# A four-engine state-space kernel: more products on POOL, a convolution tap and ScalarE's long pieces in other places

## What is computed

```python
h = layernorm(x) * (1 + ca) + sa
h, gate = split(h @ in_proj.T)                     # 2 x 1024 channels
h = silu(conv1d_causal(h, 4 taps) + conv_b)
dt, B, C = split(h @ x_proj.T)                     # 128, 16, 16
dt = softplus(dt @ dt_proj.T + dt_b)
A = -exp(A_log)
s[t] = s[t-1] * exp(dt[t] * A) + dt[t] * h[t] * B[t]     # for 1024 x 16 states
y = (sum over n of s[t] * C[t] + h * D) * silu(gate)
x = x + ga * (y @ out_proj.T)
x = x + gb * ((layernorm(x) * (1 + cb) + sb) @ sum(factors) / sqrt(8) + bias)
```

## Time and profile before

| | |
|---|---|
| device time, 3 runs | 2012.16, 2017.43, 2019.25; median 2017.43 us |
| the profiled execution | 2014.19 us, its span 2012.5 us |
| DVE busy | 1861.3 us, 92%, 2219 instructions |
| POOL busy | 1823.4 us, 91%, 757 instructions |
| PE busy | 1768.9 us, 88% |
| ACT busy | 1537.4 us, 76% |
| DMA | 93 GB/s in the mean, 16 engines under a third busy |

### The profile page before, as it was taken

One profiled execution on the slowest core, in us unless ns is written; L12 is line 12 of the kernel. 1 busy time (PEld: TensorE's weight loads), 2 busy tenths in 40 slices (PEclk: granted clock), 3 DMA queues, 4 the chain that ended last, 5 costly groups with the idle time before them and its releaser, 6 DMA issues. The chain is left out here.

```text
span 2012.5 us, 29641 instructions
## 1 busy us (share of the span) xinstructions
PE 1768.9 (88%) x9128; PEld 1316.4 (65%) x9128; DVE 1861.3 (92%) x2219; ACT 1537.4 (76%) x4897; POOL 1823.4 (91%) x757
## 2 busy tenths in 40 slices
PE   7986888989888898988989898898988889898798
PEld 5665757667576765757666675766757676575664
DVE  2798999999999999999999999999999999999995
ACT  3766778797877869778787877878787786977763
POOL 1789999999999999999999999999989999999993
PEclk9897999999999999999999999999999999999899
DMA  5655514032140412304042240403214041220300
GB/s 172 236 121 148 148 42 157 22 126 74 52 138 24 140 47 95 105 22 157 22 143 68 111 137 26 157 22 127 73 58 132 28 139 46 95 79 23 126 27 32
DMA packets 72003, 186.19 MB, mean 93 GB/s; under 512 B 6818, under 2 KB 8482, under 8 KB 63908
## 3 DMA queue, kind: packets, MB, share of 16 engines
q1 hardware_dynamic: 68148, 176.95, 25.8%
q0 software_dynamic: 3696, 7.34, 2.2%
HBM read 172.20 MB, written 12.06 MB: 92 GB/s over the span
## 5 line engine op out<-in xcount | busy, mean ns | idle before, releaser
L596 POOL TENSOR_TENSOR ub<-u,b_all 128x2048 f32<-128x2048 f32 x255 | 1167.8, 4579 | 47.1 <-DMA b_all<-bc_scratch 47.1
L752 ACT ACTIVATE decay<-dt,decay_rate 128x256 f32<-128x256 f32 (+1 forms) x2048 | 880.7, 465 | 6.0 <-DVE state_p L1503 5.4
L1503 DVE TENSOR_TENSOR_SCAN decay<-decay,carry,ub 128x512 f32<-128x512 f32 x589 | 735.5, 1275 | 11.5 <-ACT decay L752 10.5
L614 POOL TENSOR_TENSOR state_p<-state_p,c_all 128x1024 f32<-128x1024 f32 (+1 forms) x256 | 529.8, 2070 | 103.3 <-ACT carry L736 79.0
L1503 DVE TENSOR_TENSOR_SCAN state_p<-decay,carry,ub 128x512 f32<-128x512 f32 x435 | 538.3, 1269 | 38.9 <-ACT decay L752 38.4
L1070 PE MATMUL y_bank<-ident,sc_d 128*128 128x128 f32 x2356 | 351.6, 282 | 94.3 <-DVE sc_d L1518 94.3
L1518 DVE TENSOR_TENSOR sc_d<-decay,c_all 128x512 f32<-128x512 f32 x589 | 378.1, 677 | 13.1 <-PE y_bank L1070 4.4
L1070 PEld LDWEIGHTS y_bank<-ident,sc_d 128*128 128x128 f32 x2356 | 279.4, 145 | 143.3 <-DVE sc_d L1518 131.7
L1070 PE MATMUL y_bank<-ident,state_p 128*128 128x128 f32 x1740 | 247.1, 283 | 106.9 <-POOL state_p L614 105.3
L1070 PEld LDWEIGHTS y_bank<-ident,state_p 128*128 128x128 f32 x1740 | 204.2, 145 | 203.6 <-POOL state_p L614 148.0
L736 ACT ACTIVATE carry<-decay 128x2 f32<-128x2 f32 x589 | 96.4, 164 | 313.3 <-DVE sc_d L1518 313.3
(11 more groups left out here) (141 smaller groups left out, 1837.9 us busy)
## 6 DMA issues: line engine op xcount, KB each, us to landing
win_h<-win_m SPq DMA_DIRECT2D x128, 256.0 KB, 2.6
win_z<-win_m SPq DMA_DIRECT2D x128, 256.0 KB, 2.9
b_all<-bc_scratch SPq DMA_DIRECT2D x31, 1024.0 KB, 4.7
c_all<-bc_scratch SPq DMA_DIRECT2D x31, 1024.0 KB, 5.4
xa<-x SPq DMA_DIRECT2D x16, 512.0 KB, 5.1
xc<-x SPq DMA_DIRECT2D x16, 512.0 KB, 3.8
out<-xc SPq DMA_DIRECT2D x15, 512.0 KB, 3.8
ffn<-factors POOLq DMA_DIRECT2D x7, 1024.0 KB, 9.9
```

The costliest lines, as they stand in the source:

```text
L596: pool.tensor_tensor(ub[:, slot, :, :, :], u[:, (PAIRS * c + q) % U_PAIRS, :, :].unsqueeze(1).to_broadcast([P, QUAD, 2, ROWS]), b_all[:, n ...
L614: pool.tensor_tensor(part, part, c_all[:, n:n + k, :].unsqueeze(2).to_broadcast([P, k, 2, ROWS]), ALU.mult).then_inc(pooled, 1)
L752: last = act.activation(bk[:, j * ROWS + j:(j + 1) * ROWS], dt[:, pair % DT_PAIRS, j, j:], ACT.Exp, scale=decay_rate[:, e, n:n + 1])
L1503: dve.tensor_tensor_scan(dst, bk[:, :], ub[:, quad % UB_RING, i, :, :].rearrange("p j r -> p (j r)"), carried_in[:, n, 2 * q:2 * q + 1], A ...
```

## The change

Three things, and nothing else moves.

1. `EVERY_POOL` gives POOL two units instead of one in quads 7 and 15 of chunks 2 to 15 (28 units in all). DVE has 561 products instead of 589, and 28 of POOL's products are 128x1024 instead of 128x512.
2. In chunks 1 to 14 the two tap instructions of pair 0 stand between the two scans of step 6 instead of at the end of step 5.
3. On ACT the two instructions of `z_after` stand at either side of `decays(43)` and those of `z_before` at either side of `decays(61)`; the two calls of `modulate_after` move half a step back each, and `copy_dt` one step.

```diff
-EVERY_POOL = (2, 2, 2, 1) * PAIRS
+EVERY_POOL = (2, 2, 2, 1, 2, 2, 2, 2) * (PAIRS // 2)
...
-            def normalize(c, nrm, src, dst, chain, done):
+            def normalize(c, t, nrm, src, dst, chain, done):
                 act.wait_ge(chain, NORMS * c + NORMS)
-                for t in range(LB):
-                    last = act.activation(dst[:, t, :], src[:, t, :], ACT.Identity,
-                                          bias=nrm[:, 1, t:t + 1], scale=nrm[:, 0, t:t + 1])
-                last.then_inc(done, 1)
+                made = act.activation(dst[:, t, :], src[:, t, :], ACT.Identity,
+                                      bias=nrm[:, 1, t:t + 1], scale=nrm[:, 0, t:t + 1])
+                if t == LB - 1:
+                    made.then_inc(done, 1)
...
                     decays(2 * step)
...
-                        if s == 21:
+                        if s == 22:
                             copy_dt(c + 1)
...
+                    if lc is not None and s == 21:
+                        z_after(c - 1, 0)
                     if lc is not None and s == 23:
-                        modulate_after(c - 1, 1)
+                        act.wait_ge(mods_made, 4)
+                        modulate_after(c - 1, 0)
+                    if c + 2 < CHUNKS and s == 30:
+                        z_before(c + 2, 0)
...
                     decays(2 * step + 1)
...
                     if c + 2 < CHUNKS and s == 30:
-                        z_before(c + 2)
+                        z_before(c + 2, 1)
                     if lc is not None:
                         if s == 21:
-                            z_after(c - 1)
-                        if s == 22:
-                            act.wait_ge(mods_made, 4)
-                            modulate_after(c - 1, 0)
+                            z_after(c - 1, 1)
+                        if s == 23:
+                            modulate_after(c - 1, 1)
...
                     scan(unit)
...
+                    if la is not None and c and s == 6:
+                        taps(c + 1, 0)
...
                     scan(unit + 1)
...
-                        if a in TAP_AT[c > 0]:
+                        if a in TAP_AT[c > 0] and (c == 0 or s != 5):
                             taps(c + 1, TAP_AT[c > 0][a])
```

More of the change, by code:

```diff
@@ L769, in modulate, with z_before @@
                 return last
-            def z_before(c):
-                normalize(c, nrm_a, xa, xa, norm_a, z_a)
+            def z_before(c, t):
+                normalize(c, t, nrm_a, xa, xa, norm_a, z_a)
             def modulate_before(c, j):
@@ L921, in tanh_gate_last, with z_after @@
                 act.activation(tanh_s[:, :], bank_a[q % 2][:, :], ACT.Tanh, scale=0.5).then_inc(tanh_g_made, 1)
-            def z_after(c):
-                if c + 2 < CHUNKS:
+            def z_after(c, t):
+                if t == 0 and c + 2 < CHUNKS:
                     act.wait_ge(tapped, PAIRS * (c + 3))
-                normalize(c, nrm_c, xc, z2, norm_c, z_c)
+                normalize(c, t, nrm_c, xc, z2, norm_c, z_c)
             def modulate_after(c, j):
@@ L947, in _ @@
             act.activation(cond_s[:, :, :], cond[:, :, :], ACT.Tanh, scale=0.5).then_inc(cond_tanh, 1)
-            z_before(0)
+            for t in range(LB):
+                z_before(0, t)
             act.wait_ge(consts_made, 2)
@@ L1006, in one_round @@
                         if c == 0 and s == 3:
-                            z_before(1)
+                            for t in range(LB):
+                                z_before(1, t)
                         if a == M_AT[c > 0]:
```

## The result

The changed kernel takes **2029.51 us** in the median of 5 runs (2026.95 to 2030.8); the kernel before, 2014.84 in the median of 5 (2012.16 to 2019.25). The ratio is 1.0074, 95% interval 1.0062 to 1.0085: 0.7% slower. The forecast was 2026.6 us, +9.2 us of change against the +14.7 that the medians now show. The profiled execution has a span of 2027.8 us, 15.3 more than the one of before. TensorE's mean granted clock is 0.955 of full speed there, 0.969 before.

A forecast was written before the change was run, and what follows sets the result against it. A loop of waits over POOL, PE, ACT and DVE bounds the kernel, no single engine. Terms +17.0, -9.2 and +1.4 sum to +9.2 us: 2026.6 us against the median 2017.43, 0.46% slower; range 2020 to 2032.

The forecast's parts named there:

- What ends last: DVE's scan of unit 12 hangs on POOL's product of quad 15, over PE and ACT; DVE's way ends within 0.09 us.
- A: Stretch from POOL's product of quad 12 at step 26 to DVE's scan of unit 12: claimed +1.42 us, 12 times.
- first rival: POOL's product isn't what ends last; DVE's way decides, each chunk shrinks by 1.50 us: 1998 us, chance 0.17.
- B: Stretch from DVE's scan of unit 12 to POOL's next product of quad 12: claimed -0.71 us, 13 times.
- B, the tap, +0.78: Between unit 12's scan and step 8, the tap no longer runs inside DVE's wait for the decay: +0.78 us a chunk.
- second rival: The tap is free because some other DVE wait moves behind step 6: 2016.5 us, no difference, chance 0.20.
- Quad 7, -0.62: Around steps 14 to 16, DVE loses unit 29's product, saving 0.79 us, of which 0.62 come through packed PE.
- ACT, -0.87: In steps 22 and 23, DVE's waits of 0.69 and 0.18 us for decays go: -0.87 us a chunk.
- third rival: ACT's gain doesn't come while both costs stay, since `copy_dt` lies behind unit 44's decay: 2038 us, chance 0.10.
- last stretch: After chunk 14's product of quad 12: +2.16 us for POOL's longer products, less 0.79 for unit 61's: +1.4.
- gate: POOL's product of quad 12 at step 26, which waits 1.68 us for DVE's scans; the forecast's loop starts there.
- The signs: Profile after: POOL idle near 5.2 us, PE's quad 15 wait about 2.6, unit 12 wait 3 to 4, chunks 120.0.

The follow-up runs named there:

- quad 15 alone: The kernel before with POOL's second unit only in quad 15 of chunks 2 to 15: 2049.3 us, ratio 1.0163.
- spare work: From chunk 1 PE turns a tile of zeros 58 times a chunk where it otherwise waits: kernel before 2012.9 us with it, changed kernel 2022.3 us.
- ScalarE with quad 7: The kernel before with ACT's new order and POOL's second unit in quad 7 only: 2016.3 us; with useless PE turnings in its waits 1998.6 us.
- the tap's kernel with spare work: The kernel before with the moved tap, plus useless turnings of zeros in PE's waits: 2024.0 us, ratio 1.0036; the tap alone took 2035.3 us.

## Why the prediction came out as it did, step by step

**What ends last.** Confirmed. POOL's product of quad 15, PE, ACT, then DVE's scan of unit 12 set A: the longer product moved A by its own length and PE's four more turnings, and real work put into PE's wait gave 1.11 us back. The first rival (1998) is out.

**A, +1.42.** Measured +1.45 to +1.47, in the changed kernel and with quad 15 alone. The assumption that `z_before`'s halves cost 0 holds in the changed kernel only, where the longer POOL product covers them; without it they cost 0.25.

**B, the tap, +0.78.** Measured +0.78; the second rival (the tap is free) is out. **Quad 7, -0.62:** measured -0.59. **ACT, -0.87:** measured -1.00; the 0.87 are the two waits that went, and the other 0.13 us I haven't traced. The third rival (ACT's gain doesn't come) is out. B is -0.81 instead of -0.71.

**The counts and the last stretch.** From chunk 1's gate to chunk 14's the forecast was 17.0 - 9.2 = +7.8; the profiled executions show +11.3 (1564.87 against 1553.56 us), with four times 1.68 for the clock in them. Two terms were put at 0 and weren't: up to chunk 1's gate the profiled execution took 1.3 us less (297.95 against 299.25), and A into chunk 2 took 42.93 instead of 43.79; I haven't traced either. The last stretch was the term most out: +1.4 forecast, +5.3 measured. PE's rows in chunk 15 split it, counted from the gate. Up to PE's wait in step 24 it is 2.07 us longer, near the 2.16 of POOL's two products. The work right behind that wait takes 5.12 instead of 3.60 us (1972.20 to 1977.32, 1960.13 to 1963.73), +1.52, with the clock at its lower level from 1971.92 to 1975.33. And from PE's last wait for DVE (ahead of 1974.94 before, of 1988.53 after, 2.52 and 2.53 us) PE works without a pause up to 1994.07 and 2009.35, in 20.82 instead of 19.13 us, +1.69, with the lower level from 1988.99 to 1992.40. The same four products in it, before and after:

```profile
1975.87 1.88 PE L1289 MATMUL bank_c<-wo,yg 128*128 128x512 f32 x4
```

```profile
1989.89 3.13 PE L1295 MATMUL bank_c<-wo,yg 128*128 128x512 f32 x4
```

2.07 + 1.52 + 1.69 = 5.28. So 3.2 us of this term are the clock, and the 0.79 that the forecast took off for unit 61's product didn't come. Other kernels bear out the second fall: in the seven that have one near step 29 of chunk 15, 29.6 to 30.9 us pass from the last scan to the end, in the other seven 27.9 to 29.0. Spare work didn't prevent it in the changed kernel (the last stretch is 164.1 us there). What stays open is why the kernel before takes 161.6 us with spare work, 1.9 more than without.

**The signs.** POOL's idle time (5.2), the tap right behind the scan, the lost waits in steps 22 and 23 and chunks near 120.0 came as written; only chunk 2 was below 119.3, with 118.4 (119.3 before). PE's wait for quad 15 is 2.19 us at 804.15, but 0.99 at 684.14, where PE came late by the lower clock; 2.6 was expected. The wait at unit 12 is 2.08 us, not 3 to 4, because DVE waits 1.07 us earlier, in step 2, for PE to turn one of its products.

**What was missing.** The argument read PE's granted clock once, as a mean of the whole run, and then took PE's row lengths as fixed. They are fixed only as long as PE's waits stay where they are. The undisturbed stretches give 12 x 1.45 - 13 x 0.81 + 2.07 = +8.9 us, and with spare work on both sides the change costs +9.1; both bear out the +9.2 of the sum. By stretch the profiled executions with spare work differ by -0.5 us up to chunk 1's gate, +6.8 from there to chunk 14's and +2.5 in the last stretch (forecast 0, +7.8 and +1.4), so single terms are off by about 1 us and partly cancel. The other 5.6 us of the measured 14.7 have no term. The forecast came near the measured time because before and after both happen to lose nothing to the clock in most chunks. For each of the four parts alone the same way of working gave a time 9 to 12 us too short (2049 for 2037, 2016 for 2007, 2035 for 2025, 2013 for 2004). (For quad 15 alone that even counted 1.67 us for each chunk with a fall near step 0, as the changed kernel had shown it.) So the mechanism and the sum were right, and that 2026.6 came so near 2029.5 was also a matter of luck.

## What to carry to other kernels

Read PE's granted clock at each of its waits, not as a mean, and ask of each lower stretch whether slack or the path lies under it: an edit elsewhere that shifts waits by a microsecond can move it from one to the other, and make good edits look useless (ScalarE with quad 7: no gain as they are, 0.9% with the clock held). Where a kernel's PE stands still for a microsecond or two at a time, fill those waits with harmless products first, and judge other edits only then. And compare edits by their stretch between two fixed points of the loop, in the chunks where the clock doesn't fall, rather than by total times: B added up to the last digit that way, the times didn't (+50 us against +14.7).

## What the runs showed of the hardware

PE at its lower clock (granted 0.53 to 0.57 in the stretches shown, whose ends lie a little outside the fall) needs 3.55 us for eight 128x256 products that take 2.00 otherwise. The fall comes behind waits of PE (2.19 us ahead of 804.15; 1.52 and 0.89 ahead of 593.89 and 595.87), and the same two waits bring it at different places: behind 595.90 in chunk 4, ahead of the input projection, and behind 356.50 in chunk 2, on it. Turning a tile of zeros 8 times took 1.04 us by the row, and 0.87 where the next piece followed at once (594.40 to 595.27 in the tap's kernel with spare work). With 58 a chunk, A and B of the kernel before stayed at 42.33 and 77.01, and with the tap the clock was 1.00 over whole chunks.
